# Identity products on TensorE where it would wait: first tiles of the experts, of wide attention and of the last phase

## The reference, cut to what matters

```python
x = x + _L0_attn_ref(_layernorm(x), ...)                  # 16 heads of 8, causal
x = x + _L0_xattn_ref(_layernorm(x), ctx_1024, ctx_1024, ...)   # 16 heads of 8, with a context
x = x + _L0_ffn_ref(_layernorm(x), ...)                   # 8 experts, top 2, hidden 512, silu(gate)*up
x = x + _L1_attn_ref(_layernorm(x), ...)                  # 16 heads of 64, rope, causal
x = x + _L1_xattn_ref(_layernorm(x), ctx_1024, ctx_1024, mask)  # one head of 128, padded keys
x = x + _L1_ffn_ref(_layernorm(x), ...)                   # 352 hidden, inputs, weights and hidden quantised
```

## Time and profile before

| | us |
|---|---|
| median of 3 runs | 1160.22 |
| lowest and highest of them | 1157.81, 1162.24 |
| the profiled execution, its own time | 1151.02 |
| its span | 1149.2 |

### The profile page before, as it was taken

The page is one execution under the profiler, slowest core; times in us unless marked ns, Lnnn a source line. Parts: engine busy times, 40 slices in busy tenths (PEclk is TensorE's granted clock), DMA queues, the critical chain, the costliest instruction groups (busy, mean ns, idle before and its releaser), DMA issues. The chain is left out here.

```text
span 1149.2 us, 38657 instructions
## 1 busy us (share of the span) xinstructions
PE 993.0 (86%) x14756; PEld 799.4 (70%) x14759; DVE 846.6 (74%) x2027; ACT 588.4 (51%) x982; POOL 562.9 (49%) x705
## 2 busy tenths in 40 slices
PE   5999999999945799999937999999999999778554
PEld 2666666667632799999936888888888888655113
DVE  5878787888749344444418989999999998578676
ACT  3665656677730566666612444444444444366545
POOL 4232424353300533333126888888888877433104
PEclk9999999999965899999968999999999999955555
DMA  8200000000000111111130000000000000050002
GB/s 257 101 2 0 2 11 20 21 20 28 11 28 0 45 47 48 48 46 48 39 108 13 12 13 11 9 11 11 11 11 9 11 9 1 11 138 20 1 0 74
DMA packets 36984, 37.60 MB, mean 33 GB/s; under 512 B 7142, under 2 KB 31145, under 8 KB 36522
## 3 DMA queue, kind: packets, MB, share of 16 engines
q1 hardware_dynamic: 31690, 27.33, 7.9%
q0 software_dynamic: 4352, 8.92, 3.1%
q10 hardware_dynamic: 866, 0.33, 0.1%
HBM read 27.65 MB, written 8.91 MB: 32 GB/s over the span
## 5 line engine op out<-in xcount | busy, mean ns | idle before, releaser
L1283 POOL DMA_INDIRECT e_x<-xn_rows,e_where x72 | 68.2, 947 | 162.5 <-DVE e_where L1264 114.7
L360 POOL TENSOR_SCALAR n_KX<-n_KT,n_of_head 128x512 f32<-128x512 f32 x124 | 83.8, 697 | 122.1 <-ACT n_KT L601 85.2
L1253 DVE COPY e_y<-e_Y_ps 128x128 f32<-128x128 f32 x72 | 21.0, 292 | 112.5 <-PE e_Y_ps L1220 112.5
L760 DVE TENSOR_REDUCE n_row_max<-n_S_ps 128x16 f32<-128x1024 f32 x64 | 78.1, 1221 | 26.3 <-PE n_S_ps L451 26.3
L1440 POOL TENSOR_TENSOR a_E<-a_E,a_rsum 128x512 f32<-128x512 f32 x64 | 66.6, 1041 | 53.8 <-DVE a_rsum L1804 53.7
L665 ACT ACTIVATE n_ET<-n_ET_ps 128x1024 f32<-128x1024 f32 x64 | 65.5, 1023 | 46.5 <-PE n_ET_ps L461 45.8
L461 PEld LDWEIGHTS n_ET_ps<-ident,n_E 128*128 128x128 f32 x512 | 57.1, 142 | 34.9 <-issue 20.1
L764 DVE TENSOR_TENSOR n_E<-n_S_ps,n_row_max 128x1024 f32<-128x1024 f32 x64 | 78.4, 1225 | 2.9
L1210 PE MATMUL e_G_ps<-e_xT,e_gate_here 128*128 128x128 f32 x576 | 77.2, 278 | 0.0
L1210 PE MATMUL e_U_ps<-e_xT,e_up_here 128*128 128x128 f32 x576 | 76.9, 277 | 0.0
L1688 ACT ACTIVATE a_OT<-a_VQ_ps 128x512 f32<-128x512 f32 x64 | 38.2, 597 | 75.4 <-PE a_VQ_ps L1584 75.4
(11 more groups left out here) (280 smaller groups left out, 2674.3 us busy)
## 6 DMA issues: line engine op xcount, KB each, us to landing
slot_out<-e_y SPq DMA_DIRECT2D x72, 64.0 KB, 1.5
X<-in_x SPq DMA_DIRECT2D x8, 256.0 KB, 5.4
n_ctxT<-in_ctxT SPq DMA_DIRECT2D x8, 256.0 KB, 3.2
m_gate_w<-in_L_ffn_gate_w SPq DMA_DIRECT2D x1, 2048.0 KB, 7.4
m_up_w<-in_L_ffn_up_w SPq DMA_DIRECT2D x1, 2048.0 KB, 13.4
m_down_w<-in_L_ffn_down_w SPq DMA_DIRECT2D x1, 2048.0 KB, 17.7
xn_rows<-n_xn SPq DMA_DIRECT2D x8, 256.0 KB, 2.2
t_ctxT<-in_ctxT SPq DMA_DIRECT2D x8, 256.0 KB, 3.4
```

Source lines behind the costliest of these rows:

```text
L360: last = nc.gpsimd.tensor_scalar(KX[:, p, :, h * T:(h + 1) * T], src, of_head[:, h:h + 1], 1.0, ALU.mult, ALU.mult)
L760: nc.vector.tensor_reduce(row_max[:, u % 2, :], src, AX.X, ALU.max).then_inc(max_done, 1)
L1283: nc.gpsimd.indirect_dma_start(out=x[:, j, :], out_offset=None, in_=k.xn_rows, in_offset=bass.IndirectOffsetOnAxis(ap=where[:, j, :], axis ...
```

## The change

A helper `keep_warm` issues a number of products of `identb` with itself, each overwriting the same 128 columns of a bank that nobody reads at that time. `turn_identity` does the same as a PE transpose of `identb`. Neither waits for anything nor signals anybody; all other instructions stay as they were.

```diff
+def keep_warm(nc, k, bank, count):
+
+    for _ in range(count):
+        nc.tensor.matmul(bank, k.identb[:], k.identb[:], start=True, stop=True)
...
             pe.wait_ge(w_loaded, 48)
+            keep_warm(nc, k, Y_ps[1][:, 0:P], 40)
             turn_x(0, 0)
...
             def prologue():
+                keep_warm(nc, k, Y_ps[:, 0:P], 90)
                 pe.wait_ge(weights, 16 * N_WEIGHTS)
                 transpose_x(0)
...
                     project_k(0, g)
                     if g == 1:
+                        keep_warm(nc, k, Y_ps[:, 0:P], 32)
                         scores(0, 0)
+                keep_warm(nc, k, Y_ps[:, 0:P], 32)
...
+            def turn_identity(count):
+                for _ in range(count):
+                    nc.tensor.transpose(T_ps[1][:, 0:P], k.identb[:], k.identb[:])
+
+            turn_identity(60)
             transpose_x(0)
+            turn_identity(24)
             pe.wait_ge(pad_ready, 1)
             scores(0)
             transpose_x(1)
             for blk in range(NB):
                 if blk + 1 < NB:
                     scores(blk + 1)
+                if blk <= 3:
+                    turn_identity(10)
                 transpose_e(blk)
                 if blk + 2 < NB:
                     transpose_x(blk + 2)
+                if blk <= 3:
+                    turn_identity(10)
                 weigh_values(blk)
```

## The result

| | before | changed |
|---|---|---|
| median, us | 1159.38 (1155.39 to 1163.99, 15 runs) | 1155.03 (1153.02 to 1158.14, 15 runs) |
| profiled execution: span, mean granted clock | 1149.2, 0.899 | 1153.4, 0.916 |

The ratio is 0.9968, interval 0.9954 to 0.9982: 3.7 us faster (the two medians are 4.4 apart), inside the half per cent that I had called "the same". It looks like case A with its 2.8. It isn't: the experiments show that the gain had another source than the clock in its larger part.

A forecast was written before the change was run, and what follows sets the result against it. PE bounds the experts; in the last phase's attention PE is slow at a low clock with DVE close behind. Gains of 1.8 + 0.6 + 0.4 = 2.8 us take 1160.2 to 1157.4, whole range 1151 to 1165.

The forecast's parts named there:

- the same: Whole kernel: a change within half a per cent, 5.8 us, can't be told from none; given 0.66.
- case A: Whole kernel, likeliest (0.54): gains of 1.8 in experts, 0.6 in wide attention, 0.4 in last phase; 2.8 us, to 1157.4.
- Experts: 40 products before the first tile raise the clock early: 1.8 us gained, bounds -0.1 and 2.0.
- the gap that I feared: Experts, 379.1 to 380.39: PE has only one transpose to do, so the raised clock may not stay.
- First fill of wide attention: 90 products end 4.6 to 6.8 us before real work at 600.33; low clock again, no gain.
- Two fills of 32: Wide attention: delay hidden, full clock around 620 removes DVE's 1.63 us wait; 0.6 gained, bounds 0 and 1.6.
- Next POOL is late: Wide attention: POOL's division at 625.52 stands behind four gathers without idle time, and DVE's next maxima hang on it.
- The 0.6: Wide attention, second item: the part of DVE's 1.63 us wait for queries counted as gained, in us.
- Last phase: Attention of the last phase, 60, 24 and per-block transposes: 0.4 us gained, bounds 1.3 gained and 6.0 lost.
- up and down: Last phase, four blocks: the clock alternates, since PE's work fills some two thirds of DVE's period once fast.
- After it DVE is the bound: Last phase blocks: DVE's maxima are 6.49 us apart, PE's masks only 5.44 at the low clock.
- Rival C: Identity transposes don't raise the clock: last phase loses 6.0, other places gain 2.4; 3.6 us slower, 1163.8; chance 0.17.

The follow-up runs named there:

- changed kernel's third profile: The changed kernel, unedited, run and profiled once more against the kernel before: ratio 0.9955, experts 209.52 us, wide attention 414.86 us.
- second profile of the changed kernel: The changed kernel, unedited, run and profiled again against the kernel before: ratio 0.9941, experts 209.43 us, wide attention 415.01 us.
- 4 products: The kernel before with only 4 identity products added at the start of the plan phase: ratio 0.9985.
- 16 products: The kernel before with only 16 identity products added at the start of the plan phase: ratio 1.0002.

## Why the prediction was right, and where not

**Experts: right, in mechanism and size.** Forecast 1.8 gained, between -0.1 and 2.0. Measured 211.6 to 211.8 without any of the 40 (210.9 with them in the plan phase) against 209.4 to 209.5 in the five profiles that have them and no standstill, so 2.0 to 2.4: at the upper bound or a little over it. The working took 0.86 of 1.71 from the lengths of records; by the distances it is 1.71 - 0.90 = 0.81. The 40 products take 3.7 to 4.0 us. The rise came sooner after the first product than the 4.1 to 4.8 us that I carried over: in the first profile at 379.4, 3.0 us after 376.39. That it might not stay did not come true through the gap that I feared; only the standstill of the first profile brought it down, at 393.1.

**First fill of wide attention: right in outcome, in its sizes by chance.** No clock gain, and the low clock at the first product, as forecast. The idle time of 5.85 us lies within my 4.6 to 6.8 only because the fill was interrupted by its three pauses, 2.7 us together. I had it begin at the low clock and last 6.9 to 9.2 us; it began at the high one. In the changed kernel's third profile it began so too, had no pause, lasted 5.2 us and left 9.1 us of idleness; in the second it began low, lasted 7.8 and left 6.3. The first projection was slow in all three.

**Two fills of 32: the delay was hidden as forecast, the gain failed.** The step was "What they buy is a full clock around 620: DVE's wait of 1.63 us for queries at 622.16 goes". In the changed kernel the wait stayed, as the clock fell at 625.2, before that place; with the two fills alone it moved to the keys. PE still stands for 2.4 us behind the fills, waiting for POOL's division, and no product is placed there. The doubt that I wrote down behind the step, "Next POOL is late", was the right one: POOL's division and DVE's next maxima come no sooner (6.42 and 8.33 us, 6.40 and 8.32 before), whatever becomes of the wait. The 0.6 is 0.

**Last phase: gain 0.1 to 0.4 in three profiles, where I had 0.4.** The wait of 1.29 us shrank to 0.94 only, because the clock had fallen at 1017.7, while PE waited 1.87 us for `t_ctxK`, a transfer. Block 0 ran at the low clock; from 1024.5 on it was full through blocks 1 to 3, better than "up and down", and that bought next to nothing: the step "After it DVE is the bound" held. Alone this part can't be told from nothing (0.9995).

**Rival C fell.** 60 bf16 transposes of the identity and nothing else ran from 1007.77; the clock was 0.50 at 1009 and rose at 1010.9. Each of the ten from 1026.43 took (1027.00 - 1026.43) / 10 = 0.057 us at the full clock, where I had 0.053 (half of 0.102 is 0.051). The Trainium skill, "TensorE: Matmul & The Clock Gate", Part 4, says that transpose mode doesn't engage the full clock. These rows contradict it, if `nc.tensor.transpose` sets that mode, which the records don't tell; the measurement decides.

**What the prediction lacked** is the largest term, and it stood at nothing without a reason. All its steps asked which real product runs at which clock; none asked what 358 more instructions do to those behind them. The clock accounts for 2.1 + 0.2 = 2.3 us. The place of the code accounts for 416.7 or 420.6 less 415.0, so 1.7 to 5.6 us by the profiles. The ratio of the 40 in the plan phase, over many executions, tells it more exactly: (1 - 0.9965) x 1154.4 = 4.0 us, of which 0.8 lies in the experts by its profile, so 3.2 to 4.0. Together that is 5.5 to 6.3; the medians of the second and third comparison of the changed kernel differ by 6.8 and 5.8.

**Why the first comparison gave only 3.7** stays half open. Its profile has the standstill, which costs 216.32 - 209.5 = 6.8 us, and 1155.18 less 6.8 is 1148.4, what the other two comparisons show. But the kernel before was slower there too, 1159.4 against 1154.4. Its cause isn't known. In the second profile of the changed kernel another queue that carries instructions (q14) delivers a packet at 387.5; in the first, none between 376.5 and 393.5. In all others one comes 11 to 14 us behind the start of the experts, in this one only after 17. Whether that is cause or effect can't be told. The standstill came back in none of the twelve further profiles. It seems to belong to that comparison and not to one execution of it: all 15 executions of the changed kernel took 1153.0 us or more there, all 13 later ones 1151.0 or less. The kernel before was slow there too: its 15 executions took 1155.4 or more, while its profiled one had taken 1151.0. So the 3.7 us say less of the change than the later ratios do.

So the number was right by luck in good part: A's 2.8 held some 0.8 that didn't exist and lacked 3 to 4 that did, of which the first comparison then hid a share.

**A better version?** The experts' 40 alone: 0.9944, as good as the changed kernel's 0.9941 and 0.9955, with 318 instructions fewer.

## What to carry to other kernels

Raising the clock ahead of a dense stage pays only where PE itself is what is waited for and work stands ready when it is up; that was so at one place of four. Before a gain of under one per cent is put down to an edit, put the same number of harmless instructions at a place where the edit's mechanism can't work: here this control gave 4.0 of some 6 us, 0.8 of them in the experts. And where PE has pauses that wait for nothing, in code that runs for the first time, look at the queue that carries instructions, and try a few lengths of padding ahead.

## What was not expected of the hardware

- The place of PE's code is worth up to 5.6 us of 420 in a phase whose work is untouched, and it doesn't seem to be monotonic: 4 products 416.9, 16 products 418.4, 40 to 90 products 414.6 to 416.1 us, one profile each, with ratios of 0.9985 and 1.0002 for the first two, whose intervals just touch.
- The time from the first dense product to the rise of the clock varies from one execution to the next. In the experts it was 3.0 us behind the fill of the changed kernel and 4.1 in the kernel before. With 40 products in the plan phase, when PE had stood idle in between, it was only 2.6: products from 382.51, and the window 385 to 386 shows 0.94. A rise 1.5 us sooner is worth half of that, 0.75 us, which is what its experts gained. In the fill of 90, begun at the low clock, it came after 2.9 us with the 90 alone (590.54 to 593.4) and after 5.5 in the changed kernel's second profile (586.00 to 591.5). A plan for the clock that needs it within 1 us is not to be had from one profile.
- The time from PE's last dense work to the fall varied too: 2.3 us ahead of wide attention before and in the changed kernel at 625.2, 3.5 with the two fills of 32 alone, where PE had taken up work again at 620.85, and 0.7 in the changed kernel at 1017.7.
- Products of an identity, 127 of 128 elements zero in each row, count for the clock like any other work.
